# A graph transformer layer on one core: the mix layer's feed-forward half moved from the table stage into the edge batches

## The chip, the core and the metric

The kernel runs on one core of a Trainium2 chip. The metric is the device time of one launch in microseconds (us). Engines are named as in the profile: PE (TensorE; PEld is its weight load), DVE (VectorE), ACT (ScalarE), POOL (GpSimd), and SP, whose queue issues most DMAs. All data is fp32 but for index rows and one-hot matrices.

## What is computed

A layer over 3125 nodes of width 256 and 50,000 edges with 3 edge types and 6 node types. It adds to x a typed graph attention (softmax over all edges of a type, messages summed by target node) and a "mix" branch with linear attention, and then a small feed-forward with a gate by top-k. Of the mix branch (xn is the layer-normed x, q, k, v its projections, D = 256):

```python
x1 = layer_norm(t + x, ln1_g, ln1_b)                    # t: linear attention
h = gelu(einsum('nfc,oc->nfo', x1, W1) + b1, approximate=False)
y = einsum('nfc,oc->nfo', h, W2) + b2
return layer_norm(y + x1, ln2_g, ln2_b)
...
x = x + gnn(xn) + mix(xn)
x = x + ffn(layernorm(x))
```

## The kernel before, in words

Nodes are worked in NT = 25 tiles of 128, type-sorted nodes in NS = 30 slots, edges (sorted by target) in NB = 49 batches of two groups (NG = 98 groups) of four tiles of 128. All engines have their own instruction stream, written out by hand, and meet by counted semaphores (`seen`, `at_least`, `wait_ge`). The profiled execution falls into stages:

- 0 to 80 us: layer norm of all nodes, sums over keys for the linear attention.
- 80 to 292 us, the table stage: a software pipeline over NS + 1 slots. A slot projects one slot's keys, values and queries and writes them to tables in HBM, and takes one node tile (`m`) through the mix branch at lags of 0 to 5 slots. On PE (from L1010) the order is mix_q, keys_values (L921), mix_t, mix_turn, queries (L932), mix_h (L985), turn_in (L896), by_type (L909), mix_y (L1006, L1007). ACT runs elu, affine, gelu (L794), DVE residual and finish, with the second layer norm (L1299 to L1314), POOL the roots and `gained` (L667). SP stores the finished row to `mix_scratch`. The exponential of `elu` (L776) and the gelu use different activation tables, so ACT loads tables in between.
- 292 to 920 us, the edge stage. Batch b, engine by engine: POOL gathers the key and value rows of source nodes, 4 indirect DMAs a group (L1425), into a ring of RING = 7 slots; a slot is free again when the sums of its group are done. PE spreads query rows to edges (L1604), sums messages over windows of targets (L1621), turns sums (L1630) and adds totals (L1639). ACT runs keep_sums, distances, keep_rows (L1522), exponentials (L1513), onehots (L1500). DVE multiplies queries and keys (L1750), sums over heads (L1757), takes maxima, and multiplies values by weights (messages, L1809). SP loads key rows and query windows, `keys(b + 1)`, `q_window(2b)`, `q_window(2b + 1)`.
- 920 to 984 us, the close: window sums are scaled (DVE L2062), multiplied (PE L2315), kept (ACT L2250) and stored by SP (L2138) in 17 units k; SP also loads the mix rows by `load_part(k + 2)` (L2105), two tiles at a time. POOL gathers the tails and, early, the first five node tiles' sums (L2203). `keep` has two buffers.
- 984 us to the end: the final layer norm, gate and feed-forward, on PE L2351 and L2364; DVE's `with_rows(i)` adds the mix row to the gathered sums.

Constants of the close: HALF_AT = 5, EARLY_AT = 8, EARLY = 5. The weights `wmix` (W1 and W2 of the mix branch) were overwritten as the ring's seventh slot in the edge stage.

Of the kernel before, what the change touches and what calls it, by code (L numbers as in the profile page):

```python
# [26 lines left out]
EG = 4  # L27
# [5 lines left out]
RING = 7  # L33
RING_BIG = RING - 1
# [9 lines left out]
SEARCH_AT = 6  # L44
SEARCH_STEPS = 4 + NT + 4
# [30 lines left out]
def build(nc, a, out):  # L76
# [13 lines left out]
    with ExitStack() as ctx:  # L90
# [62 lines left out]
        edge = Arena("edge", 7808)  # L153
# [95 lines left out]
        kv_slots = [kv[:, s, :, :] for s in range(RING_BIG)] + [wmix[:, :].rearrange("p (k d) -> p k d", k=EG)]  # L249
# [62 lines left out]
        same_t = [vecs[name][0:HW, 0:NHG] for name in ("L0_mix_ln2_g", "L0_mix_ln2_b")]  # L312
        base_f = vecs["L0_mix_b2"][:, 0:NHG + 1]
# [152 lines left out]
        with nc.Block() as block:  # L466
            @block.sync
            def _(sp):
# [2167 lines left out]
```

## Time and profile before

| | |
|---|---|
| median of 3 timed runs | 1048.76 us (1048.03 to 1049.56) |
| the profiled execution, own span | 1167.3 us |
| PE busy in it | 967.1 us (83%) |
| DVE | 803.3 us (69%) |
| POOL | 640.5 us (55%) |
| ACT | 587.4 us (50%) |
| granted PE clock | 0.99 or above to 292 us and from 984 us, 0.66 from 340 to 900 us |

Busy shares are means over the stages above, which have different limits. A busy engine is one that executes; time in a wait for a semaphore is idle. The chain of waits follows the last instruction back to what released it. The timed runs and the profiled execution are different executions of the same program.

### The profile page before, as it was taken

How to read it: one execution, taken by the hardware profiler on the slowest of the kernel's cores; microseconds unless marked ns; L12 is line 12 of the kernel's file. 1: busy time of each engine (PE TensorE's matmuls, PEld its weight loads, DVE VectorE, ACT ScalarE, POOL GpSimd, SP SyncE). 2: the span in 40 equal slices, each digit the busy share in tenths (PEclk: the TensorE clock that was granted, in tenths of full speed). 3: DMA queues.
4: the chain of work that ended last, by engine and by line, in shares of the span. 5: the costliest groups of instructions: out<-in, count | busy, mean ns of one | idle time of the engine just before them, and what ended most of it. 6: DMA issues, size and time to landing. Idle time of an engine off the chain costs nothing.

```text
span 1167.3 us, 18084 instructions
## 1 busy us (share of the span) xinstructions
PE 967.1 (83%) x5053; PEld 677.5 (58%) x5053; DVE 803.3 (69%) x1708; ACT 587.4 (50%) x1534; POOL 640.5 (55%) x818
## 2 busy tenths in 40 slices
PE   5989999997157788777877878778778898999998
PEld 4767777775034444444444444444444687888886
DVE  7755888885256777777767677776767677887541
ACT  2657999983234554555545455554555322322220
POOL 4516788886725666666656666565664025664000
PEclk9999999999565766666667666666776799999999
DMA  9722544444736776766767767677674274210020
GB/s 294 220 71 104 159 145 145 146 146 174 234 114 182 208 212 210 205 204 203 214 202 214 210 198 211 201 211 208 201 211 146 69 226 152 79 46 19 1 86 25
DMA packets 112091, 189.89 MB, mean 163 GB/s; under 512 B 18187, under 2 KB 80734, under 8 KB 111990
## 3 DMA queue, kind: packets, MB, share of 16 engines
q0 software_dynamic: 38992, 129.87, 36.1%
q1 hardware_dynamic: 69718, 55.57, 15.7%
q10 hardware_dynamic: 3280, 3.28, 0.8%
q8 instruction: 43, 0.70, 0.2%
q14 instruction: 58, 0.48, 0.1%
HBM read 154.21 MB, written 34.44 MB: 162 GB/s over the span
## 4 chain that ended last, share of the span: by engine, by line
PE 55%; ACT 12%; issue 11%; another core or an unknown queue 10%; DVE 9%; DMA 1%; SPq 1%; POOL 0%; DVEq 0%; ACTq 0%; POOLq 0%
PE ps L2364 7%; PE ps L1621 7%; PE ps L2351 7%; PE ps L1604 6%; PE ps L921 4%; ACT edge L1500 4%; PE ps L2315 3%; PE ps L932 2%; PE ps L909 2%; PE ps L960 2%; ACT edge L1488 2%; PE ps L985 2%; ACT edge L1485 1%; PE ps L1639 1%
## 5 line engine op out<-in xcount | busy, mean ns | idle before, releaser
L1425 POOL DMA_INDIRECT big<-kv_scratch,src_i x336 | 317.8, 946 | 203.0 <-issue 89.8
L1604 PE MATMUL ps<-edge 64*128 64x256 f32 x784 | 177.6, 595 | 39.0 <-issue 38.8
L1750 DVE TENSOR_TENSOR big<-big,ps 128x1024 f32<-128x1024 f32 x84 | 101.6, 1210 | 121.3 <-PE ps L1604 61.9
L1621 PE MATMUL ps<-big,edge 128*64 128x256 f32 x672 | 149.4, 590 | 19.3 <-issue 10.3
L1604 PEld LDWEIGHTS ps<-edge 64*128 64x128 f32 x784 | 104.7, 289 | 89.5 <-issue 75.1
L1522 ACT ACTIVATE edge<-ps 128x256 f32<-128x256 f32 x98 | 37.6, 383 | 213.3 <-remote 146.0
L1621 PEld LDWEIGHTS ps<-big,edge 128*64 128x64 f32 x672 | 63.2, 199 | 78.6 <-issue 70.0
L1500 ACT ACTIVATE edge<-edge 128x64 f32<-128x64 f32 x392 | 102.9, 334 | 0.0
L1757 DVE TENSOR_REDUCE ps<-big 128x32 f32<-128x1024 f32 x84 | 102.3, 1218 | 0.1
L1809 DVE TENSOR_TENSOR big<-big,ps 128x1024 f32<-128x1024 f32 x84 | 98.9, 1209 | 0.0
L2351 PE MATMUL ps<-big 128*128 128x256 f32 (+2 forms) x416 | 88.7, 368 | 2.8 <-ACT big L2264 2.8
L2364 PE MATMUL ps<-big 128*128 128x256 f32 (+1 forms) x400 | 90.0, 380 | 0.0
L2277 ACT ACTIVATE big<-ps,fb 128x256 f32<-128x256 f32 (+2 forms) x104 | 39.4, 461 | 99.8 <-PE ps L2351 99.8
L1630 PE MATMUL ps<-ident,edge 128*128 128x128 f32 x196 | 53.6, 365 | 41.2 <-ACT edge L1522 32.7
L2351 PEld LDWEIGHTS ps<-big 128*128 128x128 f32 x416 | 74.3, 190 | 11.8 <-ACT big L2264 2.7
L2364 PEld LDWEIGHTS ps<-big 128*128 128x128 f32 (+1 forms) x400 | 73.6, 188 | 10.6 <-issue 0.3
L1425 POOL DMA_INDIRECT wmix<-kv_scratch,src_i x56 | 53.1, 948 | 30.8 <-issue 15.0
L1488 ACT ACTIVATE edge<-edge,ones 128x256 f32<-128x256 f32 x98 | 49.8, 508 | 29.4 <-remote 20.3
L1630 PEld LDWEIGHTS ps<-ident,edge 128*128 128x128 f32 x196 | 23.4, 168 | 68.7 <-ACT edge L1522 51.3
L921 PE MATMUL ps<-big,edge 128*128 x120 | 56.9, 596 | 0.5 <-ACT edge L727 0.3
L1485 ACT ACTIVATE edge<-edge,iota_n 128x256 f32<-128x256 bf16 x98 | 48.7, 497 | 13.9 <-DMA edge<-key_scratch 13.8
L1504 ACT ACTIVATE edge<-edge,ones 128x256 f32<-128x256 f32 x98 | 49.8, 508 | 8.9 <-issue 0.4
(354 smaller groups left out, 1919.0 us busy)
## 6 DMA issues: line engine op xcount, KB each, us to landing
edge<-q_scratch SPq DMA_DIRECT2D x196, 64.0 KB
edge<-key_scratch SPq DMA_DIRECT2D x98, 64.0 KB
big<-kv_scratch,src_i POOLq DMA_INDIRECT x336
agg_scratch<-big SPq DMA_DIRECT2D x16, 252.0 KB
xn_scratch<-big ACTq DMA_DIRECT2D x5, 640.0 KB, 5.4
mix_scratch<-big SPq DMA_DIRECT2D x25, 128.0 KB
big<-xn_scratch SPq DMA_DIRECT2D x25, 128.0 KB, 2.6
edge<-in_x SPq DMA_DIRECT2D x24, 128.0 KB
```

The source lines that it names most:

```text
L921: ins = pe.matmul(ps[1][:, :], xgT[:, t.k, ch * P:(ch + 1) * P], wall[:, ds(ty, 1), ch, 0:2 * D].rearrange("p a o -> p (a o)"), start=(ch ...
L1425: pool.indirect_dma_start(kv_slots[s][:, k, :], None, kv_d[0:N, :], bass.IndirectOffsetOnAxis(ap=src_i[:, e:e + 1], axis=0)).then_inc(got[ ...
L1488: act.activation(ohT[:, g % 2, :], dist, ACT.Relu, bias=ones[:, 0:1], scale=-1.0).then_inc(oh, 1)
L1500: ins = act.activation(gap[:, 2 * k + hg, :], iota_m, ACT.Abs, bias=neg_key[:, e:e + 1])
L1604: ins = pe.matmul(qr_ps[g % 2][:, (2 * hg + k) * D:(2 * hg + k + 1) * D], ohT[64 * hg:64 * hg + 64, g % 2, k * P:(k + 1) * P], qwin[64 * h ...
L1621: ins = pe.matmul(sums_of(g)[64 * hg:64 * hg + 64, :], oneh[:, s, k, hg * 64:hg * 64 + 64], kv_slots[s][:, 2 * hg + k, D:2 * D], start=(k ...
L1630: ins = pe.transpose(sums_of(g)[:, ch * P:(ch + 1) * P], rows_of_sums(g)[:, ch * P:(ch + 1) * P], ident[:, :])
L1750: dve.tensor_tensor(k_rows, k_rows, qr_ps[g % 2].rearrange("p (k d) -> p k d", d=D), ALU.mult).then_inc(pr, 1)
L1757: dve.tensor_reduce(scr[:, g // 2 % 2, (g % 2) * EG * H:(g % 2 + 1) * EG * H].rearrange("p (k h) -> p k h", h=H), kv_slots[g % RING][:, :, ...
L1809: dve.tensor_tensor(v, v, wgt[:, g // 2 % 2, (g % 2) * EG * H:(g % 2 + 1) * EG * H] .rearrange("p (k h d) -> p k h d", h=H, d=1).to_broadc ...
L2351: ins = pe.matmul(hslot[q % 2][:, j * GT * P:j * GT * P + w], fw1[:, ch, f * P:(f + 1) * P], cols[:, ch, at:at + w], start=(ch == 0), stop ...
L2364: ins = pe.matmul(ps[4 + t % 2][0:m, 0:D], fh[:, p % 2, f, at:at + m], fw2[:, f, :], start=(f == 0), stop=(f == FJ - 1))
```

## The change

The mix branch's second half leaves the table stage. There the stage now stops at x1 (stored transposed to `x1_d` by SP) and at x plus the norm offsets (`with_x`). RING goes from 7 to 6, so that `wmix` keeps W1 and W2 through the edge stage. For tile m, MF = 8 + 3m//2: SP loads x1 (at b = MF + 2 of its own loop, which runs ahead of the others); at the end of batch MF PE computes h; in batch MF + 1 ACT runs the gelu ahead of `keep_rows`, PE computes y and adds x1 by matmuls with the identity, and DVE adds b2 and takes statistics and gain between the messages; then SP stores x2 to `x2_d`. Nothing else is run behind the gelu. In the close SP loads x2 again, two tiles behind each unit's stores, and POOL scales it by its root and adds it to `rows` (`prepare_row`): rows 0 to 11 first, 12 to 15 after the first tails, 16 to 24 after the five early gathers. `with_rows` waits for `rp`. The diff, cut:

```diff
-RING = 7
-RING_BIG = RING - 1
+RING = 6
+RING_BIG = RING
...
+MIX_FROM = [8 + 3 * m // 2 for m in range(NT)]
...
         seen(sp, m_out, t)
         sp.dma_start(mix_d[t.t * P:(t.t + 1) * P, :], mo[:, t.k, :]).then_inc(m_st[t.k], 16)
+        seen(sp, m_x1, t)
+        sp.dma_start(x1_d[t.t, :, :], x1T[:, t.t % 3, :]).then_inc(m_x1st[t.k], 16)
...
-        roots(m.at(-5), m_c, m_r2, 1)
-        gained(m.at(-2))
...
-        gelu(m.at(-3))
...
-        mix_h(m.at(-3))
         turn_in(t.at(1))
         by_type(t.at(-1))
-        mix_y(m.at(-4))
...
-    def residual(t):
+    def with_x(t):
         if t is None:
             return
-        seen(dve, m_y, t)
-        seen(dve, m_out, t.at(-2))
-        seen(dve, m_xg, t)
-        cm(dve.tensor_tensor(x2m[:, t.k, :], ps[6][:, 0:D], x1g[:, t.t % 3, :], ALU.add))
-        cm(dve.tensor_tensor(x2m[:, t.k, :], x2m[:, t.k, :], vecs["L0_mix_b2"][:, :], ALU.add))
-        cm(dve.bn_stats(sts[:, 2 + t.k, :], x2m[:, t.k, :]))
-        dve.bn_aggr(mvs[:, 2 + t.k, :], sts[:, 2 + t.k, :]).then_inc(m_c, 1)
-
-    def finish(t):
-        if t is None:
-            return
-        seen(dve, m_c, t)
-        cm(dve.scalar_tensor_tensor(x2m[:, t.k, :], x2m[:, t.k, :], mvs[:, 2 + t.k, 0:1], vecs["L0_mix_ln2_g"][:, :],
-                                    ALU.subtract, ALU.mult))
         seen(dve, m_xin, t, 16)
-        cm(dve.tensor_tensor(xr[:, t.k, :], xr[:, t.k, :], vecs["L0_mix_ln2_b"][:, :], ALU.add))
-        seen(dve, m_r2, t)
         seen(dve, m_st, t.at(-2), 16)
-        dve.scalar_tensor_tensor(mo[:, t.k, :], x2m[:, t.k, :], rss[:, 2 + t.k, 0:1], xr[:, t.k, :],
-                                 ALU.mult, ALU.add).then_inc(m_out, 1)
+        dve.tensor_tensor(mo[:, t.k, :], xr[:, t.k, :], vecs["L0_mix_ln2_b"][:, :], ALU.add).then_inc(m_out, 1)
 
     for s in range(NS + 1):
         t, m = Tile(s // 2, s % 2, NS), Tile(s // 2, s % 2, NT)
-        residual(m.at(-5))
         ty = kv_out(t.at(0))
         elu(m.at(0))
         q_bias_in(t.at(0), ty)
         attend(m.at(-1))
-        finish(m.at(-5))
+        with_x(m.at(-2))
         shift(m.at(-1))
...
+h_ps_e, y_ps_e = ps[0][:, 0:D], ps[0][:, D:2 * D]
+
+def mix_tiles(b, lag):
+    return [m for m in range(NT) if MIX_FROM[m] + lag == b]
...
+    def load_x1(m):
+        at_least(sp, yp, m - 1)
+        sp.dma_start(x1e[:, m % 2, :], x1_d[m, :, :]).then_inc(x1in[m % 2], 16)
+
+    def store_x2(m):
+        sp.wait_ge(yg, m + 1)
+        sp.dma_start(x2_d[m * P:(m + 1) * P, :], x2e[:, m % 2, :]).then_inc(x2st[m % 2], 16)
...
         q_window(2 * b)
         q_window(2 * b + 1)
+        for m in mix_tiles(b, 2):
+            load_x1(m)
+        for m in mix_tiles(b, 4):
+            store_x2(m)
...
+    def mix_gelu(m):
+        act.wait_ge(hp, m + 1)
+        at_least(act, yp, m)
+        for j in range(C):
+            ins = act.activation(hTe[:, j * P:(j + 1) * P], h_ps_e[:, j * P:(j + 1) * P], ACT.Gelu,
+                                 bias=b1c[:, j:j + 1])
+        ins.then_inc(hk, 1)
+
...
         keep_sums(2 * b - 4)
         if b >= 0:
             distances(2 * b + 2)
+        for m in mix_tiles(b, 1):
+            mix_gelu(m)
         keep_rows(2 * b - 3)
...
+    def mix_h(m):
+        pe.wait_ge(x1in[m % 2], 16 * (m // 2 + 1))
+        at_least(pe, yr, m)
+        for o in range(C):
+            for ch in range(C):
+                ins = pe.matmul(h_ps_e[:, o * P:(o + 1) * P], w1T[:, ch, o * P:(o + 1) * P],
+                                x1e[:, m % 2, ch * P:(ch + 1) * P], start=(ch == 0), stop=(ch == C - 1))
+        ins.then_inc(hp, 1)
+
+    def mix_y(m):
+        pe.wait_ge(hk, m + 1)
+        for ch in range(C):
+            pe.matmul(y_ps_e, hTe[:, ch * P:(ch + 1) * P], w2T[:, ch, :], start=(ch == 0), stop=False)
+        for ch in range(C):
+            ins = pe.matmul(y_ps_e[:, ch * P:(ch + 1) * P], x1e[:, m % 2, ch * P:(ch + 1) * P], ident[:, :],
+                            start=False, stop=(ch == C - 1))
+        ins.then_inc(yp, 1)
+
...
         turn_sums(2 * b - 3)
+        for m in mix_tiles(b, 1):
+            mix_y(m)
         totals(b - 1)
         target_rows(2 * b + 2)
         window_sums(2 * b - 2)
+        for m in mix_tiles(b, 0):
+            mix_h(m)
     target_rows(NG - 1)
...
+    def mix_row(m):
+        dve.wait_ge(yp, m + 1)
+        at_least(dve, x2st[m % 2], 16 * (m // 2))
+        dve.tensor_tensor(x2e[:, m % 2, :], y_ps_e, vecs["L0_mix_b2"][:, :], ALU.add).then_inc(yr, 1)
+
+    def mix_stats(m):
+        dve.wait_ge(yr, m + 1)
+        dve.bn_stats(x2s, x2e[:, m % 2, :]).then_inc(ya, 1)
+
+    def mix_var(m):
+        dve.wait_ge(ya, m + 1)
+        dve.bn_aggr(x2v[:, m, :], x2s).then_inc(yv, 1)
+
+    def mix_gain(m):
+        dve.wait_ge(yv, m + 1)
+        dve.scalar_tensor_tensor(x2e[:, m % 2, :], x2e[:, m % 2, :], x2v[:, m, 0:1], vecs["L0_mix_ln2_g"][:, :],
+                                 ALU.subtract, ALU.mult).then_inc(yg, 1)
...
         mark(b)
+        for m in mix_tiles(b, 1):
+            mix_row(m)
         messages(2 * b - 2)
+        for m in mix_tiles(b, 1):
+            mix_stats(m)
         messages(2 * b - 1)
+        for m in mix_tiles(b, 1):
+            mix_var(m)
+            mix_gain(m)
         if b >= SEARCH_AT:
...
+    def load_x2(t):
+        if t >= NT:
+            return
+        at_least(sp, rp, t - 1)
+        sp.dma_start(x2e[:, t % 2, :], x2_d[t * P:(t + 1) * P, :]).then_inc(x2in[t % 2], 16)
...
+    for i in range(2):
+        sp.wait_ge(x2st[i], 16 * ((NT + 1 - i) // 2))
+    load_x2(0)
+    load_x2(1)
...
+        load_x2(2 * k + 2)
+        load_x2(2 * k + 3)
...
+    def prepare_row(t):
+        if t >= NT:
+            return
+        pool.wait_ge(x2in[t % 2], 16 * (t // 2 + 1))
+        x2 = x2e[:, t % 2, :]
+        pool.tensor_scalar(x2, x2, x2r[:, t:t + 1], None, ALU.mult).then_inc(x2g, 1)
+        pool.wait_ge(mix_in[t // 2 % 3], 16 * (t // 6 + 1))
+        pool.wait_ge(x2g, t + 1)
+        pool.tensor_tensor(rows[:, t, :], rows[:, t, :], x2, ALU.add).then_inc(rp, 1)
+
+    pool.wait_ge(yv, NT)
+    pool.tensor_scalar(x2v[:, :, 1], x2v[:, :, 1], EPS_LN, None, ALU.add).then_inc(s_x2r, 1)
+    pool.wait_ge(s_x2r, 1)
+    pool.tensor_tensor(x2r, x2v[:, :, 1], nhalf[:, :], ALU.pow).then_inc(s_x2r, 1)
+    pool.wait_ge(s_x2r, 2)
+    for t in range(2 * (HALF_AT + 1)):
+        prepare_row(t)
     pool.wait_ge(s_zst, 32)
...
     load_tails(0)
+    for t in range(2 * (HALF_AT + 1), 2 * EARLY_AT):
+        prepare_row(t)
     pool.wait_ge(sc_first, EARLY_AT)
     pool.wait_ge(sc_second, EARLY_AT)
     pool.wait_ge(s_earlyst, 16)
     for t in range(EARLY):
         gather(t)
+    for t in range(2 * EARLY_AT, NT):
+        prepare_row(t)
...
     def with_rows(i):
+        dve.wait_ge(rp, i + 1)
         dve.wait_ge(r3, 2 * i + 2)
...
-    dve.wait_ge(mix_in, 16 * len(MIX_PARTS))
```

## Rows read from the trace of the kernel before

**Rows 1.** Windows: busy us (xinstructions) by engine, PEclk, DMA, GB/s

```profile
80.00:292.00 212.00, 201.70 (x1304) 156.18 (x1303) 156.76 (x443) 169.65 (x336) 158.27 (x216) 0.99 0.41 143
...
340.00:900.00 560.00, 442.52 (x1998) 247.40 (x2000) 406.21 (x590) 295.21 (x876) 347.24 (x372) 0.66 0.68 203
...
984.00:1168.00 184.00, 176.07 (x856) 153.39 (x854) 109.73 (x372) 45.29 (x122) 58.67 (x104) 0.99 0.15 46
```

**Rows 2.** Chain of waits, steady slot, table stage: start us, us, what

```profile
155.71 1.72 PE ps L921 x4
...
158.99 0.89 PE ps L985 x8
...
161.00 0.63 PE ps L1006 x2
...
162.95 0.43 PE ps L921
```

**Rows 3.** Timeline of one edge batch: start us, us, what, idle before

```profile
623.24 1.22 DVE L1750 TENSOR_TENSOR big<-big,ps 128x1024 f32<-128x1024 f32 x1 [2.32 <-remote]
...
627.75 0.36 ACT L1513 ACTIVATE edge<-edge 128x192 f32<-128x192 f32 x1 [0.66 <-issue]
...
628.47 0.95 POOL L1425 DMA_INDIRECT big<-kv_scratch,src_i  x1 [0.30 <-issue]
...
635.10 0.38 ACT L1522 ACTIVATE edge<-ps 128x256 f32<-128x256 f32 x1 [4.17 <-remote]
635.10 1.22 DVE L1750 TENSOR_TENSOR big<-big,ps 128x1024 f32<-128x1024 f32 x1 [3.11 <-remote]
```

**Rows 4.** Costliest groups of the page: the gathers of edge rows

```profile
L1425 POOL DMA_INDIRECT big<-kv_scratch,src_i x336 | 317.8, 946 | 203.0 <-issue 89.8
```

**Rows 5.** Chain of waits in a slot without h and y, table stage

```profile
91.65 1.72 PE ps L921 x4
...
94.93 0.72 issue
...
98.03 1.72 PE ps L921 x4
```

**Rows 6.** Instruction groups of DVE: busy us, mean ns, idle before

```profile
L1308 DVE SCALAR_TENSOR_TENSOR big<-big,v_L_mix_ln_g 128x256 f32<-128x256 f32 x25 | 11.5, 460 | 0.0
...
L1300 DVE TENSOR_TENSOR big<-big,v_L_mix_b 128x256 f32<-128x256 f32 x25 | 10.7, 428 | 0.9
...
L1302 DVE BATCH_NORM_AGGREGATE big<-big 128x2 f32<-128x6 f32 x25 | 4.6, 183 | 0.9
```

**Rows 7.** Instruction groups of ACT: gelu and its table loads

```profile
L794 ACT ACT_TABLE_LOAD x22 | 28.2, 1283 | 0.4
...
L794 ACT ACTIVATE big<-ps,b1c 128x128 f32<-128x128 f32 x50 | 15.7, 365 | 3.3 <-PE ps L985 2.9
```

**Rows 8.** DMA issues of the page: KB each, median us to landing

```profile
big<-xn_scratch SPq DMA_DIRECT2D x25, 128.0 KB, 2.6
```

**Rows 9.** Instruction groups of POOL, shapes apart

```profile
L667 POOL TENSOR_TENSOR big<-big,v_L_mix_ln_g 128x256 f32<-128x256 f32 x25 | 18.0, 719 | 0.1
```

**Rows 10.** Timeline of SP's queue in the close stage

```profile
929.55 0.34 SPq L2138 DMA_DIRECT2D agg_scratch<-big  x1
...
932.19 0.33 SPq L2138 DMA_DIRECT2D agg_scratch<-big  x1
```

**Rows 11.** Timeline of ACT in the close stage

```profile
959.41 0.38 ACT L2250 ACTIVATE big<-ps 126x256 f32<-126x256 f32 x1 [4.17 <-DMA agg_scratch<-big]
```

**Rows 12.** Timeline of PE at the end of the close stage

```profile
984.49 3.62 PE L2364 MATMUL ps<-big 128*128 128x256 f32 x16
```

**Rows 13.** One POOL line: ns min/median/max, first and last start

```profile
L2213 POOL TENSOR_TENSOR big<-big,nhalf x50: 567/594/1336, 964.5 to 1074.5; 128x1 f32<-128x1 f32 x50
```

**Rows 14.** Timeline of ACT in a steady slot of the table stage

```profile
156.75 1.28 ACT L776 ACT_TABLE_LOAD   x1
...
158.05 0.42 ACT L776 ACTIVATE big<-big 128x256 f32<-128x256 f32 x1
```

More of the change, by code:

```diff
@@ L152, in build @@
         big = Arena("big", NG * C * 2 * KW + RING_BIG * EG * 2 * D)
-        edge = Arena("edge", 7808)
+        edge = Arena("edge", 7992)
         rows_1 = big.take(NT, D + 1)
@@ L248, in build @@
         kv = big.take(RING_BIG, EG, 2 * D)
-        kv_slots = [kv[:, s, :, :] for s in range(RING_BIG)] + [wmix[:, :].rearrange("p (k d) -> p k d", k=EG)]
+        kv_slots = [kv[:, s, :, :] for s in range(RING_BIG)]
         keyr = edge.take(KRING, P * 2).rearrange("p a b -> p (a b)").bitcast(BF16).rearrange("p (b u j) -> p b u j", u=2, j=2 * P)
@@ L261, in build @@
         gap = edge.take(4, 64)
+        base_f = edge.take(NHG + 1)
+        hTe = edge.take(D)
+        x2s = edge.take(6)
+        assert edge.at <= NT * D + 32
         edge.reset()
@@ L287, in build @@
         rows_c = edge.take(NT, D)
+        edge.take(32)
         selT = edge.take(C, ETY, P)
@@ L299, in build @@
         junk = edge.take(NHG)
+        same_last = edge.take(NHG)
         edge.reset()
@@ L311, in build @@
         same_h = [vecs[name][0:HW, 0:NHG] for name in ("L0_mix_ln1_g", "L0_mix_ln1_b")]
-        same_t = [vecs[name][0:HW, 0:NHG] for name in ("L0_mix_ln2_g", "L0_mix_ln2_b")]
-        base_f = vecs["L0_mix_b2"][:, 0:NHG + 1]
+        x2v = vecs["L0_mix_ln1_g"][:, NHG:NHG + 2 * NT].rearrange("p (t k) -> p t k", k=2)
+        x2r = vecs["L0_mix_ln1_b"][:, NHG:NHG + NT]
+        same_t = [vecs["L0_mix_ln2_b"][0:HW, 0:NHG], same_last[0:HW, :]]
         heads, tails, total = wqT, w1T, w2T
@@ L786, in affine @@
                     ins.then_inc(m_x1, 1)
-                def gelu(t):
-                    if t is None:
-                        return
-                    seen(act, m_h, t)
-                    seen(act, m_y, t.at(-2))
-                    for j in range(C):
-                        ins = act.activation(hT[:, t.k, j * P:(j + 1) * P], ps[7][:, j * P:(j + 1) * P], ACT.Gelu,
-                                             bias=b1c[:, j:j + 1])
-                    ins.then_inc(m_g, 1)
                 for s in range(NS + 1):
@@ L1343, in build @@
             s_baseT = sem("bases_turned")
+            x1in, x2st = pair("x1_in"), pair("x2_stored")
+            hp, hk, yp, yr, ya, yv, yg = (sem(n) for n in (
+                "mix_h_ps", "mix_h_gelu", "mix_y_ps", "mix_y_row", "mix_y_stats", "mix_y_var", "mix_y_gained"))
             vd, pd = sem("edge_step"), sem("edge_pool_step")
+            assert [s.num for s in table_sems] == list(range(table_sems[0].num, table_sems[-1].num + 1))
+            for s in table_sems:
+                nc.release_semaphore(s)
+            stage_no[0] += 1
             fb_a, fb_b, fb_c, fb_d, fb_e, fb_f1, fb_g = (sem(n) for n in (
@@ L1716, in _ @@
                 with pe.If(n > 1):
+                    pe.wait_ge(s_fresh, 1)
+                    settle(pe)
                     pe.wait_ge(fb_e, 1)
@@ L2024, in _ @@
                     dve.wait_ge(s_zk, 1 + 2 * C)
-            assert [s.num for s in table_sems] == list(range(table_sems[0].num, table_sems[-1].num + 1))
-            for s in table_sems:
-                nc.release_semaphore(s)
-            stage_no[0] += 1
             vc, pc = sem("vector_step"), sem("pool_step")
@@ L2035, in build @@
                 "scaled_first", "scaled_second", "rows_ps", "rows_kept"))
-            ck_st, mix_in = pair("rows_stored"), sem("mix_in")
+            ck_st, mix_in = pair("rows_stored"), [sem(f"x_rows_in{j}") for j in range(3)]
+            x2in, x2g, rp = pair("x2_in"), sem("x2_scaled"), sem("rows_prepared")
+            s_x2r = sem("x2_rstds")
             s_fw, s_head, s_tails = sem("ffn_weights_in"), pair("heads_in"), pair("tails_in")
```

72 lines of the change are left out of this document (25 added, 47 removed).

## The prediction

> **What bounds the kernel now.** I read the time by stage first [rows 1], then within each stage the stretch that repeats. The table stage (80 to 292 us) is bound by PE, busy 201.7 of 212 us: in a steady slot the chain of waits stays on PE from end to end [rows 2], 155.71 to 162.95, 7.24 us, and of it h takes .89 and the first part of y .63. The last stage (from 984) is PE's too, 176.1 of 184. The edge stage (340 to 900) is not so plain: PE 442.5 of 560 at a granted clock of 0.66, DVE 406, POOL 347, ACT 295. All have room, yet they restart together. In one batch (two groups of four edge tiles) [rows 3] DVE works from 623.24 until it idles 3.11 us before 635.10: 8.75 us without a gap. ACT idles 4.17 and starts in the same instant. POOL issues a gather each .95 + .30 = 1.25 us, eight a batch, 9.96 us with the means of [rows 4]. The batch lasts 11.86 us.
>
> The profiled execution is 1167.3 us, the median 1048.76: 118.5 us between them. The stages in which PE is busy at full clock can't shrink much, so I put most of the gap into the edge stage's 47 or so batches, 2.2 to 2.5 us each: a timed batch is about 9.5 us by that, and it can't be much under POOL's issue rate: 392 gathers [rows 4] by 1.245 us are 488 us. This is an inference; no timed run has a trace. On it I carry the terms over to the timed runs, with **9.96 us as the floor of a batch**, POOL's, and DVE second with 8.75.
>
> **What each part costs.** *Table stage, removed.* h, gelu, y, six of seven DVE operations and two on POOL go; one more store of 128 KB a tile joins SP's queue, which is short in this stage and keeps nobody waiting: nothing. A slot that has neither h nor y exists in the trace, while the pipeline fills [rows 5]: 91.65 to 98.03, 6.38 us, with .72 us of issue wait at 94.93, just where h would stand. So a part of the PE work that goes was in the shade of a wait, and a slot gains 7.24 - 6.38 = .86. By 25 tiles: **-22**. Bounds: -16 (.86 by 19, nothing where the pipeline fills and empties) and -38 (.89 + .63 by 25, if the wait at 94.93 goes too).
>
> *Edge stage, added.* Each of 25 tiles puts into one batch:
> - DVE: b2 add .43, statistics as much, aggregate .18, gain .46 [rows 6], 1.5 us.
> - ACT: two gelus of .365, overlapping to about .63, and two table loads of 1.283 (Gelu, then Exp again) [rows 7], 3.2 us. A small exponential would only have put the second load right behind the gelu; without it the load stands ahead of the next true exponential. Both are in the same row of work, so leaving it out gains at most one short activation here (.36 us).
> - PE: h .89 [rows 2], y with two more matmuls for x1 about 1.4, so 2.3 at full clock. At full clock PE's work of a batch is some 442.5 x .66 / 47 = 6.2 us; 8.5 fits into 9.96.
>
> DVE comes to 8.75 + 1.5 = 10.25, .29 above POOL. More follows from the order. The gelu stands ahead of keep_rows and of the batch's exponentials in ACT's row. ACT idles .66 us before the exponential at 627.75 [rows 3], so the exponentials come 3.2 - .66 = 2.5 us later, and totals (PE), weights, messages (DVE), window sums (PE) and y queue behind them. ACT can win some of it back: by [rows 1] it has 295.2 / 47 = 6.3 us of work a batch, so it idles over 3 us of 9.96 and might run ahead. Bounds: 0 and 2.5 in a mixed batch; I take half, 1.25, for the rows favour neither end. A mixed batch is then 8.75 + 1.5 + 1.25 = 11.5, 1.54 over the floor, by 25 = 38. Two batches in three are mixed; in the 12 between them DVE and POOL may catch up by at most 9.96 - 8.75 = 1.21, and I take .7: 8. **Edges +30**. Bounds: 0 (.29 by 25 = 7, which the other batches return) and +70 (12.75 - 9.96 = 2.79 by 25).
>
> *The ring, 7 to 6 groups.* By the order of the loops a group's slot comes free one batch before its products: of 9.96 us, 5.0 go to issuing its four gathers and about 2.6 to landing (the row of [rows 8], a load of the same size). 2.4 us are left, so it costs nothing in the steady state if batches are even; at most one group's issue, 5.0, at the end. Bounds 0 and +5, taken **+2**: the margin that is left is thin.
>
> *SP in the edge stage.* load_x1 and store_x2 stand behind q_window; the store waits for a gain that is three batches old. Nothing, covered by that age; if DVE were so late, keys and queries behind it on SP would be late too.
>
> *Close stage, added.* Rows are made on POOL, two operations each, nearest row .72 [rows 9], and x2 comes by SP into two buffers: load t waits until row t-2 is made. SP asks for two rows behind each unit's stores. A unit took 2.64 us, 929.55 to 932.19 [rows 10]. A pair of rows costs a landing of 2.6 [rows 8] plus one row's 2 x .72 (the other row's lie beside the landing): 4.04, 1.40 more. 25 rows are 12.5 pairs: +17.5; the two buffers of kept rows hide 2 x 2.64 = 5.3 of it. Rows 16 to 24 stand on POOL behind five early gathers, 5 x .95 + .3 [rows 4], and SP's loads wait for them: +5.1. **Close +17.** That SP is on the path I read from ACT: at 959.41 it had waited 4.17 us for stores to agg_scratch [rows 11], and from 984.49 [rows 12] PE is bound by nothing but itself, so what comes before goes to the end. Bounds: +8 (landings overlapped: 4 x .72 = 2.88 against 2.64, 3.0 in 12.5 pairs, and 5.1) and +28: POOL's small operation L2213 took 594 ns in the median, 1336 at most [rows 13]; with the two-input operation of a row stretched alike (.72 to 1.6) a pair is 2.6 + .72 + 1.6 = 4.92; 2.28 by 12.5 is 28.5, + 5.1 - 5.3 = 28.3.
>
> The Trainium skill (GPSIMD Engine Reference, Specifications) says that POOL shares its SBUF interfaces with VectorE and contends with its instructions of two SBUF inputs, which DVE runs all through this stage. The 1336 ns of [rows 13] agree in kind; by the page the close would be near +28, and the time 1087.
>
> **Sum.** -22 + 30 + 2 + 17 = +27: 1048.76 + 27 = **1076**; the profiled execution would be about 1194 by the same sum, less if its batches, which end on PE, take the added work beside it.
>
> **The rivals.**
> *A, faster.* Exponentials are not late, since ACT runs ahead; DVE's 10.25 is returned in the other batches; the close costs its lower end: -22 + 0 + 2 + 8 = -12, **1037**. For it: ACT's idle time, and DVE's 3.11 us in the profiled batch. Against: the gelu stands in front of the exponentials, not in that idle time, and POOL leaves no slack in the timed batch. With the close at +17 it turns at edges of +3; at +8, at +12, a mixed batch of about 10.7 us.
> *B, much slower.* At a granted clock of 0.66 (a mean between 1.2 and 2.4 GHz) PE's 8.5 us of work a batch become 12.8, and PE, not POOL, is the bound; or gathers land late with six slots. -22 + 70 + 2 + 17 = +67: **1116**.
> *C, no difference.* Edges +8, close +12: **1049**.
> *D, the slot doesn't shrink*, since ACT's or DVE's chain sets 7.24 us as well: the table stage gives nothing, +49: **1098**. Against it speaks the slot of 6.38.
> *E, a switch of table stops ACT for as long again as the load.* 4 x 1.283 + .63 = 5.8, exponentials 5.1 late, a mixed batch 15.35: 5.39 by 25 - 8 = 127, **1173**. In the trace a load starts at 156.75 and takes 1.28, and its activation starts at 158.05 [rows 14]: nothing stands between.
> The Trainium skill (ScalarE: Activation LUTs, What ACT_TABLE_LOAD costs) has 1283 ns for a load and some 1380 for a drain with it, 2.66 us a switch. The trace agrees on the load and shows no drain between load and activation.
>
> **How the numbers follow.** Chances: the forecast .58, its own range 1052 to 1115; A .24; C .06; B .08; D .02; E .02. Below 1034 lies the part of A that gains more (.08), above 1108 B, E and the top of the forecast (.12): 1034 to 1108. About 0.2% is what a measurement can tell from no change: faster by more .24, within .06, slower by more .70.
>
> **What would show it.** Right: slots of 6.4 us in the chain; two table loads in a mixed batch with the exponentials 1 to 2 us later behind them, and DVE idle ahead of weights; units of the close about 4 us apart with SP waiting for rows made, and PE's last stage starting some 17 us later by it. Wrong: edge batches as long as before, gelu and loads in ACT's idle time; close units still 2.64 us apart; slots of 7.2 us.

## The result, and the profile after

| | median, us | runs |
|---|---|---|
| before, in the same comparison | 1048.39 | 1047.73 to 1049.56 |
| after | 1378.45 | 1375.07 to 1381.33 |
| ratio | 1.314 | 95% interval 1.3115 to 1.3165 |

The change makes the kernel 330 us slower, where 27 were forecast. Its profiled execution has a span of 1377.7 us, which is close to its median. That was not so before: 1167.3 us in the trace against 1048.76. The chips of this study are of two kinds. The kernel before takes 1047 to 1050 us on some and 1168 to 1170 us on one, each time the same, and the trace of before is of the second kind. The experiments name the kind by the time of the kernel before that was measured beside them.

The stages by the windows of the trace after (columns as in [rows 1]):

```profile
80.00:292.00 212.00, 170.55 (x1041) 120.58 (x1039) 110.54 (x311) 116.30 (x265) 130.32 (x161) 0.95 0.56 187
340.00:1090.00 750.00, 445.85 (x2255) 292.46 (x2255) 416.92 (x662) 353.68 (x916) 322.65 (x344) 0.71 0.50 148
1195.00:1378.00 183.00, 175.53 (x853) 152.93 (x851) 108.61 (x369) 45.41 (x122) 58.27 (x104) 1.00 0.15 46
```

The last stage is as it was, 183 us with PE busy 175.5. The table stage has less work in the same window: PE 170.6 in place of 201.7. The edge stage now reaches beyond 1090 us, and there no engine is busy for more than six tenths of the time: PE 446 of 750, DVE 417, ACT 354, POOL 323. So something stops all of them. The waits of PE in the edge stage (us in total, times, longest) name it:

```profile
PE ps L1655 <- DMA wmix<-mix_x_scratch: 209.6, 25, 9.5
```

L1655 is `mix_h`. In each of the 25 batches that hold a tile (mixed batches) PE stands for its x1, 8.4 us in the mean. One such stop in the timeline (start us, us, what, idle before and its releaser):

```profile
608.26 1.08 PE L1605 MATMUL ps<-big,edge 128*64 128x256 f32 x8 [0.56 <-DVE big L1818]
608.33 1.30 SPq L1349 DMA_DIRECT2D edge<-key_scratch  x2
...
610.41 4.25 SPq L1340 DMA_DIRECT2D edge<-q_scratch  x4
...
614.70 0.59 SPq L1354 DMA_DIRECT2D wmix<-mix_x_scratch  x1
...
617.77 2.08 PE L1655 MATMUL ps<-wmix 128*128 128x128 f32 x8 [8.42 <-DMA wmix<-mix_x_scratch]
...
622.50 0.38 ACT L1500 ACTIVATE big<-ps 128x252 f32<-128x252 f32 x1 [11.18 <-PE ps L1614]
622.72 0.28 DVE L1795 TENSOR_REDUCE mall<-ps 24x1 f32<-24x128 f32 x1 [9.17 <-PE ps L1632]
...
624.39 0.94 POOL L1395 DMA_INDIRECT big<-kv_scratch,src_i  x1 [10.07 <-PE ps L1605]
```

PE has finished the window sums at 609.34 and would start h. The load of its x1 goes out from SP at 614.70, and h starts at 617.77, when it has landed. SP is late because the load stands at the end of its iteration: behind the key rows (608.33, issued once ACT's second `distances` of this batch has read the key rows whose buffer they take) and the four query windows that follow them, 4.25 us of issue. h stands in PE's row ahead of the next batch, so behind it ACT has idled 11.18 us, DVE 9.17 and POOL 10.07. The slot of the table stage is what was forecast (chain of waits):

```profile
155.40 1.72 PE ps L910 x4
...
161.78 1.29 PE ps L910 x3
```

155.40 to 161.78 is 6.38 us, as in [rows 5]. PE also stands as long as there, 0.72 us, where h stood; here the timeline names the wait, DVE's q_bias (L1213):

```profile
159.40 0.44 PE L885 MATMUL ps<-ident,edge 128*128 128x128 f32 x2 [0.72 <-DVE edge L1213]
```

### The profile page after: what moved, and what is told of

It is laid out like the page before. It is cut to its first block, busy times and chain, and to the rows that moved or that the text cites. A ratio compares the mean times of both kernels' runs of the same rounds, so it can differ in the third digit from the quotient of the medians.

```text
span 1377.7 us, 18266 instructions
## 1 busy us (share of the span) xinstructions
PE 958.4 (70%) x5153; PEld 699.7 (51%) x5153; DVE 783.7 (57%) x1657; ACT 603.1 (44%) x1540; POOL 653.8 (47%) x795
## 4 chain that ended last, share of the span: by engine, by line
PE 39%; issue 11%; ACT 10%; DVE 10%; SPq 10%; DMA 10%; POOL 9%; DVEq 0%; ACTq 0%; POOLq 0%
DMA wmix<-mix_x_scratch 8%; PE ps L2419 6%; PE ps L2432 6%; POOL big L1395 5%; SPq L1340 4%; PE ps L1655 4%; PE ps L1588 4%; PE ps L910 3%; SPq L1339 3%; DVE big L1818 2%; SPq L1349 2%; POOL wmix L2229 2%; PE ps L949 2%; ACT edge L1472 2%; ACT L1485 2%
## 5 line engine op out<-in xcount | busy, mean ns | idle before, releaser
L1395 POOL DMA_INDIRECT big<-kv_scratch,src_i x392 | 370.5, 945 | 435.1 <-PE ps L1605 334.2
L1655 PE MATMUL ps<-wmix 128*128 128x128 f32 x200 | 51.9, 441 | 209.6 <-DMA wmix<-mix_x_scratch 209.6
L1588 PE MATMUL ps<-edge 64*128 64x256 f32 x784 | 157.3, 536 | 16.2 <-DMA edge<-q_scratch 12.6
L1655 PEld LDWEIGHTS ps<-wmix 128*128 128x128 f32 x200 | 44.5, 328 | 224.7 <-DMA wmix<-mix_x_scratch 224.7
L1500 ACT ACTIVATE big<-ps 128x252 f32<-128x252 f32 x98 | 35.9, 368 | 278.8 <-PE ps L1614 278.8
L1605 PE MATMUL ps<-big,edge 128*64 128x256 f32 x784 | 134.9, 475 | 26.9 <-ACT big L1500 14.2
L1759 DVE TENSOR_TENSOR big<-big,ps 128x1024 f32<-128x1024 f32 x98 | 118.7, 1211 | 14.6 <-DMA big<-kv_scratch,src_i 10.0
L1766 DVE TENSOR_REDUCE ps<-big 128x32 f32<-128x1024 f32 x98 | 119.3, 1217 | 0.1
L1818 DVE TENSOR_TENSOR big<-big,ps 128x1024 f32<-128x1024 f32 x98 | 116.5, 1207 | 0.0
L1614 PE MATMUL ps<-ident,edge 128*128 128x128 f32 x196 | 54.1, 369 | 37.1 <-ACT edge L1494 35.0
L1494 ACT ACTIVATE edge<-ps 128x256 f32<-128x256 f32 x98 | 37.6, 384 | 93.5 <-PE ps L1605 93.5
L2383 PE MATMUL ps<-bd_m,big 128*126 128x128 f32 (+1 forms) x396 | 51.7, 296 | 22.5 <-ACT big L2318 21.1
L2383 PEld LDWEIGHTS ps<-bd_m,big 128*126 128x126 f32 (+1 forms) x396 | 50.3, 209 | 24.3 <-ACT big L2318 22.4
```

What stands on the lines that cost most here:

```text
L1395: pool.indirect_dma_start(kv_slots[s][:, k, :], None, kv_d[0:N, :], bass.IndirectOffsetOnAxis(ap=src_i[:, e:e + 1], axis=0)).then_inc(got[ ...
L1588: ins = pe.matmul(qr_ps[g % 2][:, (2 * hg + k) * D:(2 * hg + k + 1) * D], ohT[64 * hg:64 * hg + 64, g % 2, k * P:(k + 1) * P], qwin[64 * h ...
L1605: ins = pe.matmul(sums_of(g)[64 * hg:64 * hg + 64, :], oneh[:, s, k, hg * 64:hg * 64 + 64], kv_slots[s][:, 2 * hg + k, D:2 * D], start=(k ...
L1655: ins = pe.matmul(h_ps_e[:, o * P:(o + 1) * P], w1T[:, ch, o * P:(o + 1) * P], x1e[:, m % 2, ch * P:(ch + 1) * P], start=(ch == 0), stop=( ...
L1759: dve.tensor_tensor(k_rows, k_rows, qr_ps[g % 2].rearrange("p (k d) -> p k d", d=D), ALU.mult).then_inc(pr, 1)
L1766: dve.tensor_reduce(scr[:, g // 2 % 2, (g % 2) * EG * H:(g % 2 + 1) * EG * H].rearrange("p (k h) -> p k h", h=H), kv_slots[g % RING][:, :, ...
```

## The experiments

Those that leave out part of the computation are named as such in what was expected of them.

**1. The load of x1 one iteration earlier.**

```diff
-        for m in mix_tiles(b, 2):
+        for m in mix_tiles(b, 1):
             load_x1(m)
```

> The changed kernel, with each load of x1 put one iteration earlier in SP's loop (b = MF + 1 in place of MF + 2). Theory L (the late load is the cause): PE waits 8.4 us for x1 in each of 25 batches, 210 us; they go, and the rest of the +330 may go with them as far as it came from the same stop: between 1080 and 1168 us. Rival X (the late exponentials behind gelu and its two table loads, and the ring of 6, carry the batch): PE waits elsewhere for nearly as long, 1250 us or more.

> The changed kernel again, beside the kernel before on the chip of this study, on which the kernel before takes 1168 us. If the +330 is a stop of fixed length (PE waits 8.4 us for x1, 25 times, whatever the clock), the changed kernel takes 1216 + 25 x 6.5 to 8.4, so 1378 to 1425 us here too, and the ratio is about 1.19. If the whole ratio of 1.31 carries over, it takes 1535 us.

> The same kernel as e1_x1_sooner, so that it stands beside the others of this call on one chip. Where the kernel before takes 1168 us: 1216. Where it takes 1048 us: between 1100 and 1190; e7_small_exp took 1193 there, e6_no_gelu 1073.

> The same kernel as e1_x1_sooner. Where the kernel before takes 1048 us: if the small exponential of e7_small_exp is within 5 us, 1190; if bringing the second table load forward costs 1.3 us and more in each mixed batch, 1120 to 1160. The wait for x1 is worth 1376 less that: 190 to 260 us, of which 210 are the 25 waits of 8.4 us.

| kernel | us | before beside it | ratio (95%) |
|---|---|---|---|
| e5_as_changed | 1376.4 | 1048.2 | 1.311 (1.307 to 1.315) |
| e14_x1_sooner | 1115.2 | 1047.5 | 1.065 (1.063 to 1.067) |
| e1_x1_sooner | 1215.7 | 1168.0 | 1.042 (1.034 to 1.049) |
| e10_x1_sooner_again | 1213.5 | 1170.3 | 1.038 (1.031 to 1.045) |

Theory L holds: this one line is worth 1376.4 - 1115.2 = 261 us of the 330. e5 was run beside a kernel before of 1048 us, so it doesn't tell what its text asked of the other kind of chip. In e14's trace SP's load goes out 5.5 us ahead of h, and PE goes from the window sums to h without a pause:

```profile
568.82 0.59 SPq L1354 DMA_DIRECT2D wmix<-mix_x_scratch  x1
...
572.38 1.97 PE L1605 MATMUL ps<-big,edge 128*64 128x256 f32 x8
...
574.28 2.08 PE L1655 MATMUL ps<-wmix 128*128 128x128 f32 x8
```

The 25 waits are 210 us. Most of the rest goes with the granted clock, by the windows 340 to 700 us of the trace after and of e14:

```profile
340.00:700.00 360.00, 215.21 (x1074) 140.96 (x1074) 203.62 (x325) 171.03 (x444) 157.58 (x168) 0.70 0.52 154
```

```profile
340.00:700.00 360.00, 277.58 (x1689) 181.77 (x1687) 307.08 (x499) 266.79 (x682) 241.19 (x255) 0.88 0.78 236
```

0.70 against 0.88: PE spends more of its time at the lower of its two levels. The two profiled spans differ by 264.3 us. PE's busy time is 67.0 of it (958.4 us after, 891.4 in e14, for the same 5153 matmuls), and its idle time 197.3: the 210 us of waits less some 12 by which its other idle time is shorter. As the kernels differ in the one line, the lower clock comes of the stops; e5, on another chip, repeats it (961.1 us busy, 0.71).

**2. Each part by itself.** e15_no_second_half has the shorter table stage and the ring of six alone; e16_no_rows_made adds h, gelu and y to the edge batches; e14 adds the rows of the close.

> The kernel before with six ring slots in place of seven, nothing else changed. Predicted term: +2 us (0 to +5). If gathers then land late in every batch (rival B), 2 us or more a batch: 1140 us.

```diff
-RING = 7
-RING_BIG = RING - 1
+RING = 6
+RING_BIG = RING
```

> The changed kernel without the mix layer's second half anywhere: no h, gelu and y in the edge batches, and no rows made in the close stage (the output lacks the normed y + x1). What is left of the change is the shorter table stage and the ring of six. Predicted terms: -22 + 2, so 1028 us. If the slot does not shrink (rival D): 1050 us.

```diff
-    return [m for m in range(NT) if MIX_FROM[m] + lag == b]
+    return []
...
-    for t in range(2 * (HALF_AT + 1)):
-        prepare_row(t)
...
-    load_x2(2 * k + 2)
-    load_x2(2 * k + 3)
```

> The same kernel as e3_no_second_half, the output without the mix branch's second half. Where the kernel before takes 1048 us: the table stage's 21 us go there too, since its clock is 0.99 on both chips: 1027.

> As e1_x1_sooner, but no rows are made in the close stage: SP loads no x2, POOL scales and adds nothing (the output lacks the mix branch's second half). Its difference to e1_x1_sooner is the price of the close: predicted 17 us (8 to 28); by the two traces, first store of a unit to first matmul behind the tails, 30 us. Its difference to e3_no_second_half is the price of h, gelu and y in the edge batches: predicted 30 us (0 to 70).

```diff
-    for t in range(2 * (HALF_AT + 1)):
-        prepare_row(t)
...
-    load_x2(2 * k + 2)
-    load_x2(2 * k + 3)
...
-    dve.wait_ge(rp, i + 1)
```

> The same kernel as e4_no_rows_made (no rows made in the close, the output lacks the mix branch's second half). It gives the price of h, gelu and y in the edge batches on this chip: -22 for the table stage, +30 for the edges by the prediction, so 8 us above the kernel before.

> The same kernel as e4_no_rows_made. Where the kernel before takes 1048 us, the edge price is this less e15: predicted 30 us there (0 to 70) with DVE and POOL as the bounds; 28 us were measured where PE at 0.66 is the bound. Less e14 it gives the close, 42 us on the other chip.

| step | where before takes 1047.5 | where it takes 1168 | forecast |
|---|---|---|---|
| ring of six alone (e2) | | +0.6 (ratio 0.999, 0.995 to 1.002) | +2 |
| table stage, with the ring (e15; e3) | -19.0 (0.981, 0.979 to 0.983) | -21.2 (0.984, 0.978 to 0.991) | -20 |
| edge batches (e16 less e15; e4 less e3) | +47.5 | +27.3 | +30 |
| close (e14 less e16; e1 less e4) | +39.2 | +41.7 | +17 |
| late x1 (e5 less e14) | +261.2 | | 0 |
| sum | 328.9 of 330 | | +27 |

In e12, in another comparison on the second kind of chip, the same kernel as e4 took 1177.7 us beside 1170.3, 7.4 above it where 8 were forecast, and e10 1213.5: the close at 35.8 there. The 95% intervals of the kernels behind the second column reach some 8 us to each side (4 for e2 and e4), those behind the first 2 to 4. The terms are differences from one kernel to the next, so they add up by construction; that they make 328.9 of the 330 says only that the kernels repeat from chip to chip. The ring alone was run on the second kind only; on the first, where gathers pace a batch (part 3), its price is in the -19.0 and not known by itself.

**3. The kernel before at its faster time.**

> The kernel before, for a trace of it on the chip of this call. Ratio 1. If the chip is one on which it takes 1048 us, the granted clock of the edge stage is above the 0.66 of the recorded trace, near 0.8 to 0.85, and POOL's gathers, not PE, close a batch of about 10 us.

> The kernel before, for a trace of it on a chip where it takes 1048 us, if this call falls on one (else as e11_before_again). Theory K (the clock): the 118 us between the recorded trace and its median are PE's clock in the edge stage, 0.66 against 0.8 or more; table and last stage have the same length in both traces. Rival: they lie in late semaphores of the profiled run.

e11 took 1170.3 us and e13 1047.1. The windows of e13:

```profile
80.00:292.00 212.00, 201.59 (x1304) 156.19 (x1303) 156.84 (x443) 169.16 (x336) 158.39 (x216) 1.00 0.41 143
340.00:760.00 420.00, 321.75 (x1814) 185.17 (x1816) 371.31 (x542) 270.61 (x799) 317.96 (x336) 0.82 0.82 250
```

Theory K holds in what it says of the stages: table stage (PE 201.6 of 212) and last stage are as in [rows 1], so nearly all of the 118 us lies in the edge stage. There the granted clock is 0.82 in place of 0.66, and DVE is busy 371 of 420 us. The chain of waits from 340 to 760 us lies on POOL's gathers, L1425, for 71.7% and on "issue" for 23.3%, which in it stands between two gathers; a batch, from one L1750 to the same one of the next, takes 9.9 us, the one behind it 10.7, and DVE now waits for a landing (timeline):

```profile
558.94 1.22 DVE L1750 TENSOR_TENSOR big<-big,ps 128x1024 f32<-128x1024 f32 x1
...
563.07 1.22 DVE L1750 TENSOR_TENSOR big<-big,ps 128x1024 f32<-128x1024 f32 x1 [1.05 <-DMA big<-kv_scratch,src_i]
...
568.86 1.22 DVE L1750 TENSOR_TENSOR big<-big,ps 128x1024 f32<-128x1024 f32 x1
```

So POOL's floor of a batch, inferred in the prediction without a trace, is there.

That the clock is the cause of the 118 us isn't shown, for the slower traces show a second difference: stops of several engines at once. In [rows 3] ACT and DVE restart together at 635.10, and POOL at 635.33 (timeline). ACT's instruction there, keep_rows, waits by the code for PE's window sums alone, and these had ended at 631.65 (the PE line from that trace stands with the first point of the next section). The waits of keep_rows in the two traces from 340 to 760 us, first e11, then e13 ("remote": the profile names no releaser on this core):

```profile
ACT edge L1522 <- remote: 112.8, 29, 4.9
```

```profile
ACT edge L1522 <- PE ps L1621: 74.8, 83, 2.0
```

The 29 starts of e11 lie 2.2 us (median) behind the end of PE's latest window sums, those of e13 0.05 us. All nine traces of the second kind have waits on "remote", and none of the eleven of the first kind has one. So the rival's late semaphores are there, though not in the profiled run alone, since the timed runs of e11 are as long (1166.6 to 1176.7 us). Whether the semaphores travelled late or PE ended later than its modelled ends say, and which of stops and clock brings the other, stays open: no run changes one without the other.

**4. What the gelu costs.**

> e1_x1_sooner with Identity in place of Gelu in the edge batches: the same bias and shapes, no load of another activation table (the output has h without the gelu). Left out: 50 table loads of 1.28 us. If late exponentials carry much of the edge price (the 1.25 us a mixed batch of the prediction), it is 25 to 60 us faster than e1; if the loads lie in ACT's idle time, within 5 us of it.

```diff
-        ... h_ps_e[:, j * P:(j + 1) * P], ACT.Gelu,
+        ... h_ps_e[:, j * P:(j + 1) * P], ACT.Identity,
```

> e1_x1_sooner with a small exponential (128x1) behind each gelu, which brings the second table load forward, ahead of keep_rows. Predicted: no more than a short activation, so within 5 us of e1. If the load has a shade to stand in only where it is late (as the change has it), up to 1.3 us a mixed batch, +32 us; if it is better early, as much faster.

```diff
     ins.then_inc(hk, 1)
+    act.activation(vecs["L0_mix_ln1_g"][:, 250:251], ones[:, 0:1], ACT.Exp)
```

> e1_x1_sooner with keep_rows(2b - 3) ahead of the gelu on ACT, nothing else changed. Theory P (PE's stop before turn_sums, 1.7 us in the trace of e14 and 3.2 in that of e7, costs most, since all else queues behind it and the granted clock falls with it): the stop goes, 15 us or more faster than e14 (1115 us beside 1047.5, 1214 beside 1168). Theory Q (what counts is when the exponentials come; with this order they come later by ACT's former wait, and y keeps PE waiting instead): the same as e14 within 8 us, or slower.

```diff
+    keep_rows(2 * b - 3)
     for m in mix_tiles(b, 1):
         mix_gelu(m)
-    keep_rows(2 * b - 3)
```

| kernel | us | before beside it | ratio (95%) |
|---|---|---|---|
| e14_x1_sooner | 1115.2 | 1047.5 | 1.065 (1.063 to 1.067) |
| e6_no_gelu | 1072.8 | 1048.2 | 1.022 (1.019 to 1.025) |
| e7_small_exp | 1193.0 | 1048.2 | 1.137 (1.133 to 1.141) |
| e17_rows_kept_first | 1129.8 | 1050.2 | 1.077 (1.074 to 1.079) |

Without the two table loads (the activation itself stays, as Identity) 42 of the edge batches' 47.5 us are gone, and 5 are left for all that DVE, PE, SP and ACT's activations have more to do. The price is that of the loads, 2.6 of the 3.2 us that the prediction put in front of the exponentials. The small exponential costs 78 us, and the traces show how. In e14 the second load stands behind keep_rows (L1494), and PE waits 1.71 us for keep_rows before it turns the sums (L1614); DVE waits 1.83 for the exponentials:

```profile
579.43 1.28 ACT L1508 ACT_TABLE_LOAD   x1
...
581.24 0.38 ACT L1494 ACTIVATE edge<-ps 128x256 f32<-128x256 f32 x1
581.64 1.28 ACT L1485 ACT_TABLE_LOAD   x1
...
581.68 0.44 PE L1614 MATMUL ps<-ident,edge 128*128 128x128 f32 x2 [1.71 <-ACT edge L1494]
...
581.95 1.03 PE L1662 MATMUL ps<-wmix,edge 128*128 128x256 f32 x4
...
582.94 0.36 ACT L1485 ACTIVATE edge<-edge 128x192 f32<-128x192 f32 x1
...
583.33 0.38 DVE L1809 TENSOR_REDUCE ps<-edge 128x64 f32<-128x192 f32 x1 [1.83 <-ACT edge L1485]
```

In e7 both loads stand ahead of keep_rows. PE waits 3.22 us, and after that y (L1663) takes 1.92 us where it took 1.03: the granted clock is 0.50 from 577.8 to 583.5 us, the lower level, against 1.00 in e14 from 581.6 to 583.9, and DVE waits 2.42 for y:

```profile
574.07 1.28 ACT L1508 ACT_TABLE_LOAD   x1
...
576.01 1.28 ACT L1511 ACT_TABLE_LOAD   x1
...
577.84 0.69 PE L1615 MATMUL ps<-ident,edge 128*128 128x128 f32 x2 [3.22 <-ACT edge L1494]
...
578.32 1.92 PE L1663 MATMUL ps<-wmix,edge 128*128 128x256 f32 x4
...
581.13 0.42 DVE L1905 TENSOR_TENSOR wmix<-ps,v_L_mix_b 128x256 f32<-128x256 f32 x1 [2.42 <-PE ps L1665]
```

The batch's exponential starts as long after the first load, 3.6 us against 3.5. From 340 to 700 us the mean granted clock is 0.76, against 0.88 in e14:

```profile
340.00:700.00 360.00, 274.03 (x1438) 183.08 (x1438) 266.08 (x424) 229.55 (x600) 208.66 (x221) 0.76 0.68 203
```

So 1.5 us more of a stop, 38 us in 25 batches, became 78 while the clock fell: PE is busy 944.9 us in e7 and 891.4 in e14 for the same matmuls. On DVE most of the 78 shows as waits. mix_row, which needs y, stands ahead of the messages there, and DVE waits for it 59.1 us in e7 and 2.4 in e14:

```profile
DVE wmix L1905 <- PE ps L1665: 59.1, 25, 2.4
```

For the exponentials it waits 45.7 us, 11.3 more than in e14: 68 together. In e17 the stop in front of L1614 goes, but PE waits as long for the gelu in front of y instead, L1662, 37.6 us against the 38.5 of L1614 in e14, and DVE waits longer for the exponentials (rows of the waits, first e14, then e17):

```profile
PE ps L1614 <- ACT edge L1494: 38.5, 25, 1.7
...
DVE ps L1809 <- ACT edge L1485: 34.4, 25, 1.8
```

```profile
DVE ps L1809 <- ACT edge L1485: 46.1, 25, 2.2
...
PE ps L1662 <- ACT edge L1508: 37.6, 25, 1.5
```

The ratio is 0.012 higher, some 12 us, as Q had it, and DVE's longer wait for the exponentials is 11.7. P's forecast of a faster kernel falls: the order of keep_rows and gelu only chooses where PE stands. But as PE stands as long in both kernels, e17 doesn't test what a stop of PE costs. The length of ACT's row before the exponentials isn't all that counts either, for in e7 it is that of e14 and the kernel is 78 us slower. What the three have in common is DVE: it pays for whatever its next instruction waits for, the exponentials in e17, y in e7.

**5. The close.**

> e1_x1_sooner, but in the close stage ACT scales the row (behind a unit's kept chunks) and POOL only adds it. In the trace POOL's scaling of 128x256 takes 0.92 us alone and up to 2.8 us; the close costs 42 us here. If POOL's operations beside DVE's are what paces it, 10 to 20 us less; if landings and SP's order pace it, within 5 us of e1.

```diff
-    pool.tensor_scalar(x2, x2, x2r[:, t:t + 1], None, ALU.mult).then_inc(x2g, 1)
...
+    act.activation(x2, x2, ACT.Identity, bias=zrow[:, 0:1], scale=x2r[:, t:t + 1]).then_inc(x2g, 1)
```

> e1_x1_sooner with the rows of the close made elsewhere: SP loads x2 into four buffers, the first four ahead of the units, the others between the loads of the last stage; DVE makes each row with one scalar_tensor_tensor (0.46 us) in the last stage, which PE bounds; POOL makes none. If the close costs what it does through POOL and SP's order, nearly all of the difference between e10 and e12 goes (within 6 us of e12). If DVE's 25 x 0.46 = 11.5 us lie on the path of the last stage, it is 11 us above e12.

```diff
+    def make_row(t):
+        dve.wait_ge(x2in[t % 4], 16 * (t // 4 + 1))
+        dve.scalar_tensor_tensor(rows[:, t, :], x2b[t % 4], x2r[:, t:t + 1], rows[:, t, :], ALU.mult,
+                                 ALU.add).then_inc(rp, 1)
...
-        prepare_row(t)
```

> The same kernel as e9_rows_by_dve. Where the kernel before takes 1168 us: 1188. Where it takes 1048 us: e16_no_rows_made (1076) plus the 10 us that DVE's rows cost in the last stage, 1086.

In the trace after, SP's stores of units (L2182) and POOL's scaling (L2229; ns min/median/max, first and last start):

```profile
1099.02 0.34 SPq L2182 DMA_DIRECT2D agg_scratch<-big  x1
...
1107.34 0.42 SPq L2182 DMA_DIRECT2D agg_scratch<-big  x1
...
1145.44 0.42 SPq L2182 DMA_DIRECT2D agg_scratch<-big  x1
...
1162.15 0.42 SPq L2182 DMA_DIRECT2D agg_scratch<-big  x1
```

```profile
L2229 POOL TENSOR_SCALAR wmix<-wmix,v_L_mix_ln_b x25: 917/924/2850, 1099.1 to 1176.4; 128x256 f32<-128x256 f32 x25
```

The first unit takes 8.3 us and the first eight 5.8 in the mean, where [rows 10] had 2.64, and between 1145.44 and 1162.15 none is stored for 16.7 (in the trace of before 6.9 at the same place, 948.03 to 954.88): SP stands with a load of x2 until POOL has made the rows behind its early gathers, and ACT waits 15.84 for its buffer of kept rows:

```profile
1165.30 0.66 ACT L2318 ACTIVATE big<-ps 126x256 f32<-126x256 f32 x2 [15.84 <-DMA agg_scratch<-big]
```

POOL's scaling has one tensor input and takes 0.92 us in the median, but 2.55 to 2.81 in the first three rows and 2.85 at the longest, each time while DVE scales beside it. e8 takes this operation off POOL: its first eight units are 4.05 us apart in the mean (SP's timeline, first and ninth store below), against 4.04 forecast for a landing and a row's work, and it takes 1100.5 us, 14.7 less than e14. The other 24.5 of the 39 us stay: two landings a unit in SP's row and a longer stop at the early gathers.

```profile
834.05 0.34 SPq L2182 DMA_DIRECT2D agg_scratch<-big  x1
...
866.45 0.42 SPq L2182 DMA_DIRECT2D agg_scratch<-big  x1
```

By the stores of e14 and e16 the close splits so: the first eight units cost 24.3 us more in e14, the stop behind them 10.1, the last seven 2.5.

e9 and e18 make the rows in the last stage on DVE. There units are 2.64 us apart again:

```profile
841.91 0.32 SPq L2183 DMA_DIRECT2D agg_scratch<-big  x1
...
844.55 0.32 SPq L2183 DMA_DIRECT2D agg_scratch<-big  x1
```

e9 takes 1187.7 us beside 1170.3 (1.016, 1.009 to 1.022), 26 less than e10 of the same comparison and 10 above e12. e18 takes 1084.5 beside 1050.2 (1.032, 1.030 to 1.035); by the ratios that is 34 us less than e14 and 6 above e16. It is the fastest kernel of this study that computes all of the changed one's work, and slower than the kernel before: the table stage's 19 us don't pay for the edge batches' 47.

## Why the prediction was wrong, point by point

- **The load of x1** is the step that failed: "load_x1 and store_x2 stand behind q_window; the store waits for a gain that is three batches old. Nothing, covered by that age". That walks the store and the queue behind it, and never the load: when is it issued, and when does PE want it? The code has the answer: load m stands at the end of SP's iteration MF + 2, behind keys(MF + 3), which waits for distances in batch MF, and h stands at the end of batch MF. The trace of before has the times (its timeline): at the end of the batch of [rows 3] PE is through with the window sums at 631.65, and SP with key rows and query windows at 638.45. With 2.6 us to land [rows 8] the load would have come some 9.4 us late, an estimate from these rows; 8.4 was measured, 25 times. The term, put at nothing, was 261 us.

```profile
630.35 1.28 SPq L1393 DMA_DIRECT2D edge<-key_scratch  x2
...
630.57 1.08 PE L1621 MATMUL ps<-wmix,edge 128*64 128x256 f32 x8 [0.84 <-issue]
...
634.17 4.28 SPq L1384 DMA_DIRECT2D edge<-q_scratch  x4
```

- **The table stage**: -22 forecast, and -19.0 and -21.2 measured with the ring's share in them. The slot without h and y while the pipeline fills was the right row; 6.38 us came back to the hundredth. Rival D fell.
- **The ring**: +2 forecast, +0.6 measured on the second kind of chip, no difference; by itself not measured on the first.
- **The edge batches**: +30 forecast, 47.5 and 27.3 measured, within the bounds. The mechanism was right: what DVE and PE add is hidden or small, and ACT's two loads ahead of the exponentials are paid for, 42 of the 47.5. The term of 1.25 us of lateness was too low: the loads alone cost 1.7 us a mixed batch (42.3 by 25). That +30 lies near the 27.3 is luck, since it was worked out for batches that POOL paces, and those gave 47.5.
- **The small exponential**: "leaving it out gains at most one short activation here (.36 us)" was wrong. Leaving it out gains 78 us, 3.1 a mixed batch, since where the second load stands decides how long PE waits for keep_rows, and DVE for y behind it. That load isn't "in the same row of work" for PE, though it is for ACT.
- **The close**: +17 forecast, 39.2 and 41.7 measured, above the upper bound of 28. The unit without the stretch came out as worked (4.04 against 4.05 in e8). The stretch of POOL's operations was put at the two-input one alone, from L2213; the scaling with one tensor input was stretched as well, from 0.92 to 2.85. The Trainium skill (GPSIMD Engine Reference, Specifications) has POOL's SBUF interfaces shared with VectorE, and contention with DVE instructions of two SBUF inputs; the rows agree, and without that operation on POOL e8 is 14.7 us faster. The block behind the early gathers was put at 5.1 us; it measured 10.1 (e14 against e16). The first eight units were put at 1.40 us more each, 11.2; they cost 24.3 in e14 and 11.3 in e8.
- **The clock.** The prediction put the 118 us between trace and median into faster batches of the timed runs, and used the right floor for one. e13 shows the floor, and two differences to the recorded trace, the granted clock of the edge stage, 0.82 against 0.66, and the stops of several engines at once, which it lacks; which is the cause is open. That a stop of PE also lowers the clock behind it was in no term: beside it 210 us of stops became 261, and 38 became 78.
- **Rival E** fell: in the trace after a load starts at 602.21 and takes 1.28, and the gelu starts at 603.51. The Trainium skill (ScalarE: Activation LUTs, What ACT_TABLE_LOAD costs) adds about 1380 ns of drain to a switch; no row here has it.

```profile
602.21 1.28 ACT L1508 ACT_TABLE_LOAD   x1
...
603.51 0.63 ACT L1508 ACTIVATE edge<-ps,b1c 128x128 f32<-128x128 f32 x2
```

## What to carry to other kernels

When work is moved into a loop that runs on several queues, walk each of its loads from the instruction that frees it to the one that wants it, through all that its own queue issues ahead of it; a load at the end of the queue's iteration may be the slowest step of a batch. An engine's idle time is no place to put work if the work stands in front of what others wait for: price it at the first instruction behind it on every engine. And a stop of PE may cost more than its length: the granted clock from 340 to 700 us was 0.70 and 0.76 in the two kernels with longer stops (the changed one, e7) against 0.88 in e14. Between kernels of different work it doesn't follow the stops: the kernel before, without these stops, had 0.82 in e13. Last, look at which chip a trace is from before it is set beside a time.

## What the runs showed of the hardware

- The same program took 1047 to 1050 us on some chips and 1168 to 1170 us on another, each steady. Table and last stage are alike; in the edge stage the granted clock is 0.82 and 0.66, and 29 starts of ACT's keep_rows on the second kind (e11) lie a median 2.2 us behind the end of PE's window sums, where it is 0.05 on the first (e13).
- Stops of PE of 8.4 us, 25 of them, went with a granted clock of 0.70 where the same kernel without them had 0.88 (e14; 0.84 and 0.85 in e16 and e8, whose edge batches are the same).
- POOL's tensor_scalar of 128x256 took 0.92 us at the least and 2.85 at the most beside DVE's instructions of two SBUF inputs.
- A table load took 1.28 us, with its activation right behind.
